# A fused graph-attention and expert kernel: dense experts in the slot pass take two node blocks at a time, in halves of the inner width

## The reference

```python
h = (x_flat @ W_gat).reshape(M, HEADS, NUM_EXPERTS)
a_src = (h * att_src).sum(-1)
a_dst = (h * att_dst).sum(-1)
e = leaky_relu(a_src[src] + a_dst[dst], 0.2)          # one per edge and head
ee = exp(e - segment_max(e, dst)[dst])
agg = segment_sum(h[src] * ee / denom, dst)           # 16 numbers a node
scores = layernorm(agg + b_gat).reshape(M, 4, 4).mean(1)
topk_s, topk_i = top_k(scores, 2); w = softmax(topk_s)
for ei in range(4):                                   # dense: every node, every expert
    g = where(topk_i == ei, w, 0).sum(-1)
    hh = gelu(x @ W1[ei] + b1[ei])                    # 256 -> 512
    out = out + g[..., None] * (hh @ W2[ei] + b2[ei]) # 512 -> 256
```

## Time and profile before

| | |
|---|---|
| Median of 3 runs | 7682.64 us (7681.4 to 7688.64) |
| The profiled execution | 7684.64 us, with a span of 7682.9 us in the trace |
| Slot pass, first gather to last sums | 6160.9 to 7561.8 us of the span |
| Behind it (scores and mixing) | to the end at 7682.9 us |

### The profile page before, as it was taken

One profiled execution on the slowest core, in us unless ns is written; L12 is line 12 of the kernel. 1 busy time (PEld: TensorE's weight loads), 2 busy tenths in 40 slices (PEclk: granted clock), 3 DMA queues, 4 the chain that ended last, 5 costly groups with the idle time before them and its releaser, 6 DMA issues. The chain is left out here.

```text
span 7682.9 us, 117784 instructions
## 1 busy us (share of the span) xinstructions
PE 5447.3 (71%) x27644; PEld 4598.9 (60%) x27645; DVE 3924.1 (51%) x10109; ACT 1568.1 (20%) x3440; POOL 5707.3 (74%) x7330
## 2 busy tenths in 40 slices
PE   3888888777772599990555555555556589999993
PEld 3666666666661489880444434344435589999983
DVE  4777777888887500005454544444445533333326
ACT  1222222222220233330000000000001234444431
POOL 2888888888876577776888888888886577777762
PEclk7888888888885699995777777776777678888886
DMA  3333333333333255553333333333331133333698
GB/s 121 106 106 106 106 107 105 103 103 103 102 101 95 85 174 174 171 172 117 104 104 104 102 92 92 92 92 92 92 93 49 28 86 79 80 79 80 71 72 188
DMA packets 426071, 793.43 MB, mean 103 GB/s; under 512 B 129162, under 2 KB 267134, under 8 KB 425684
## 3 DMA queue, kind: packets, MB, share of 16 engines
q0 software_dynamic: 235504, 474.87, 26.8%
q1 hardware_dynamic: 190436, 317.20, 12.2%
HBM read 720.67 MB, written 70.98 MB: 103 GB/s over the span
## 5 line engine op out<-in xcount | busy, mean ns | idle before, releaser
L1156 PE MATMUL g_pM<-g_G,g_S 128*128 x3328 | 1196.6, 537 | 1190.0 <-ACTq L1050 1070.9
L834 POOL DMA_INDIRECT g_G<-table,X x1664 | 1611.4, 968 | 401.9 <-issue 385.6
L845 POOL DMA_INDIRECT g_G<-table,g_IDX x1616 | 1542.1, 954 | 416.7 <-issue 392.3
L1156 PEld LDWEIGHTS g_pM<-g_G,g_S 128*128 128x128 f32 x3328 | 916.0, 282 | 1470.5 <-issue 1272.4
L1124 PE MATMUL g_pM<-g_G,g_S 128*128 128x260 f32 x3328 | 1125.3, 481 | 407.5 <-DVE acc L953 400.6
L618 POOL DMA_INDIRECT slots<-sort_PAIR,sort_ADDR x1024 | 1029.1, 1005 | 415.4 <-issue 276.2
L1699 POOL DMA_INDIRECT q_G<-table,slot x1072 | 1028.3, 959 | 370.3 <-issue 320.6
L961 DVE TENSOR_TENSOR acc<-g_pM,acc 128x256 f32 x1664 | 698.4, 420 | 1005.4 <-PE g_pM L1156 1002.6
L1124 PEld LDWEIGHTS g_pM<-g_G,g_S 128*128 128x128 f32 x3328 | 706.5, 231 | 692.7 <-DVE acc L953 566.5
L953 DVE TENSOR_TENSOR acc<-g_pM,acc 128x260 f32 x1664 | 711.2, 427 | 188.8 <-PE g_pM L1124 40.4
L941 DVE TENSOR_SCALAR g_S<-iota,g_REL,g_WT 128x128 f32<-128x128 f32 x1664 | 591.2, 356 | 193.2 <-issue 172.4
(11 more groups left out here) (336 smaller groups left out, 7382.3 us busy)
## 6 DMA issues: line engine op xcount, KB each, us to landing
e_W<-in_L_ffn_W SPq DMA_DIRECT2D x210, 512.0 KB, 4.4
sort_PAIR<-slot_rows SPq DMA_DIRECT2D x66, 512.0 KB, 4.5
g_G<-table,X POOLq DMA_INDIRECT x1664
g_G<-table,g_IDX POOLq DMA_INDIRECT x1616
ys_all<-ew_Y SPq DMA_DIRECT2D x196, 128.0 KB, 1.8
sm_Y<-ys_all SPq DMA_DIRECT2D x28, 896.0 KB, 10.6
q_ST<-slot_rows SPq DMA_DIRECT2D x34, 512.0 KB
sort_ADDR<-slot_rows SPq DMA_DIRECT2D x34, 512.0 KB
```

The costliest lines, as they stand in the source:

```text
L834: pool.indirect_dma_start(G[:, r, u, :], None, table, bass.IndirectOffsetOnAxis(ap=IDX[:, k * GRP + u:k * GRP + u + 1].bitcast(U32), axis= ...
L845: pool.indirect_dma_start(G[:, r, u, :], None, table, bass.IndirectOffsetOnAxis(ap=IDX[:, g * GRP + u:g * GRP + u + 1].bitcast(U32), axis= ...
L1156: m = pe.matmul(pM[r % 2 * 2 + half][:, u % HG, :], S[:, r, u, :], rows.rearrange("p a d -> p (a d)"), start=True, stop=True)
```

## The change

A dense unit is now two blocks by one expert, done in two halves of the inner width. `by_w1` of a half covers 2 of the 4 chunks for two blocks: 4 matmuls of 256 columns, with one weight load for the two blocks. `gelu` of a half is 2 activations of 128x256. `by_w2` of a half adds its 2 chunks to both blocks' outputs, 4 matmuls of 256 columns, in one PSUM bank that holds 512 columns and is complete after the second half. `add_b2` and `store` come once for two halves, with 128x512 and 256 KB. The 49 blocks make TWOS = 25 twos; the last is blocks 47 and 48, so block 47 is computed twice and stored once. Halves stand where pairs stood: one in an even group and two in an odd one. A loop body has 16 groups with 24 halves, the loop has 7 passes where there were 15, and `REST` gives two halves to each of the first four groups of the last six.

```diff
-        self.GT = layer.sb(f"{tag}_GT", [P, 2, HC, P])
-        self.Y = layer.sb(f"{tag}_Y", [P, E, D])
+        self.GT = layer.sb(f"{tag}_GT", [P, 2, HC // 2, 2 * P])
+        self.Y = layer.sb(f"{tag}_Y", [P, E, 2, D])
...
-    def by_w1(self, pe, i, e):
-        q = i * self.E + e
-        n = len(self.pH)
-        at_least(pe, self.s["gelu"], (q + 1 - n) * self.HC)
-        for c in range(self.HC):
+    TWOS = (NB + 1) // 2
+    HALF = 2
+
+    def first_block(self, two):
+
+        return NB - 2 if isinstance(two, int) and two == self.TWOS - 1 else two * 2
+
+    def by_w1(self, pe, two, e, half):
+        q = (two * self.E + e) * 2 + half
+        at_least(pe, self.s["gelu"], (q - 1) * self.HALF)
+        for c in range(self.HALF):
+            hidden = (half * self.HALF + c) * P
+            out = self.pH[half][:, c, :].rearrange("p (a m) -> p a m", a=2)
             for k in range(KC):
-                m = pe.matmul(self.pH[e % n][:, c, :], self.W1[:, e, k, c * P:(c + 1) * P],
-                              self.XT[:, bass.ds(i, 1), k, :].rearrange("p a m -> p (a m)"), start=(k == 0), stop=(k == KC - 1))
+                m = pe.matmul(out, self.W1[:, e, k, hidden:hidden + P], self.XT[:, bass.ds(self.first_block(two), 2), k, :],
+                              start=(k == 0), stop=(k == KC - 1))
         m.then_inc(self.s["h"], 1)
 
-    def by_w2(self, pe, i, e):
-        q = i * self.E + e
-        n = len(self.pY)
-        at_least(pe, self.s["yc"], q + 1 - n)
-        pe.wait_ge(self.s["gelu"], (q + 1) * self.HC)
-        for c in range(self.HC):
-            m = pe.matmul(self.pY[e % n][:, 0:D], self.GT[:, e % 2, c, :], self.W2[:, e, c, :], start=(c == 0),
-                          stop=(c == self.HC - 1))
+    def by_w2(self, pe, two, e, half):
+        q = (two * self.E + e) * 2 + half
+        if half == 0:
+            at_least(pe, self.s["yc"], two * self.E + e - 1)
+        pe.wait_ge(self.s["gelu"], (q + 1) * self.HALF)
+        for j in range(2):
+            for c in range(self.HALF):
+                m = pe.matmul(self.pY[e % 2][:, j * D:(j + 1) * D], self.GT[:, half, c, j * P:(j + 1) * P],
+                              self.W2[:, e, half * self.HALF + c, :], start=(half == 0 and j == 0 and c == 0),
+                              stop=(half == 1 and c == self.HALF - 1), skip_group_check=True)
         m.then_inc(self.s["y"], 1)
 
-    def gelu(self, a, i, e):
-        q = i * self.E + e
+    def gelu(self, a, two, e, half):
+        q = (two * self.E + e) * 2 + half
         a.wait_ge(self.s["h"], q + 1)
         at_least(a, self.s["y"], q - 1)
-        for c in range(self.HC):
-            a.activation(self.GT[:, e % 2, c, :], self.pH[e % len(self.pH)][:, c, :], ACT.Gelu,
-                         bias=self.B1T[:, e * self.HC + c:e * self.HC + c + 1]).then_inc(self.s["gelu"], 1)
-
-    def add_b2(self, v, i, e):
-        q = i * self.E + e
-        v.wait_ge(self.s["y"], q + 1)
-        at_least(v, self.s_stored[e], i * 16)
-        v.tensor_tensor(self.Y[:, e, :], self.pY[e % len(self.pY)][:, 0:D], self.B2[:, e, :], ALU.add).then_inc(self.s["yc"], 1)
-
-    def store(self, sp, i, e):
-        sp.wait_ge(self.s["yc"], i * self.E + e + 1)
-        sp.dma_start(self.ys[bass.ds(i * P + e * NP, P), :], self.Y[:, e, :]).then_inc(self.s_stored[e], 16)
+        for c in range(self.HALF):
+            at = e * self.HC + half * self.HALF + c
+            a.activation(self.GT[:, half, c, :], self.pH[half][:, c, :], ACT.Gelu,
+                         bias=self.B1T[:, at:at + 1]).then_inc(self.s["gelu"], 1)
+
+    def add_b2(self, v, two, e):
+        v.wait_ge(self.s["y"], (two * self.E + e) * 2 + 2)
+        at_least(v, self.s_stored[e], two * 16)
+        v.tensor_tensor(self.Y[:, e], self.pY[e % 2][:, :].rearrange("p (a d) -> p a d", a=2),
+                        self.B2[:, e, :].unsqueeze(1).broadcast_to([P, 2, D]), ALU.add).then_inc(self.s["yc"], 1)
+
+    def store(self, sp, two, e):
+        sp.wait_ge(self.s["yc"], two * self.E + e + 1)
+        if isinstance(two, int) and two == self.TWOS - 1:
+            r0 = e * NP + (NB - 1) * P
+            sp.dma_start(self.ys[r0:r0 + P, :], self.Y[:, e, 1, :]).then_inc(self.s_stored[e], 16)
+        else:
+            sp.dma_start(self.ys[bass.ds(two * (2 * P) + e * NP, 2 * P), :].rearrange("(a p) d -> p a d", p=P),
+                         self.Y[:, e]).then_inc(self.s_stored[e], 16)
...
-    STEP = 2 * RINGS
+    STEP = 4 * RINGS
     FULL = SGF // STEP
     E = dense.E
-    PAIRS = [[0], [1, 2], [3], [4, 5], [6], [7, 8], [9], [10, 11]]
-    REST = [[0], [1], [2], [3], [], []]
-    NPAIR = sum(len(x) for x in PAIRS)
+    HALVES = [[n // 2 * 3] if n % 2 == 0 else [n // 2 * 3 + 1, n // 2 * 3 + 2] for n in range(STEP)]
+    REST = [[0, 1], [2, 3], [4, 5], [6, 7], [], []]
+    NHALF = sum(len(x) for x in HALVES)
...
+        def halves(it, g):
 
             if not exists(it, g):
                 return []
-            table_of = REST if isinstance(it, int) and it == FULL else PAIRS
+            table_of = REST if isinstance(it, int) and it == FULL else HALVES
             return [(it, m) for m in table_of[g]]
 
-        def block_expert(it, m):
-            return it * (NPAIR // E) + m // E, m % E
-
-        def pair_before(it, m):
-
-            return (it, m - 1) if m > 0 else (it - 1, NPAIR - 1)
+        def unit(it, m):
+            return it * (NHALF // (2 * E)) + m // (2 * E), m // 2 % E
+
+        def second(it, g):
+
+            return [unit(*half) for half in halves(it, g) if half[1] % 2 == 1]
+
+        def half_ahead(it, m):
+
+            return (it, m - 1) if m > 0 else (it - 1, NHALF - 1)
...
-                for pair in pairs(*later(it, g, -2)):
-                    dense.store(sp, *block_expert(*pair))
+                for of in second(*later(it, g, -2)):
+                    dense.store(sp, *of)
...
-                for pair in pairs(it, g):
-                    dense.by_w1(pe, *block_expert(*pair))
-                    if not (isinstance(it, int) and it == 0 and pair[1] == 0):
-                        dense.by_w2(pe, *block_expert(*pair_before(*pair)))
+                for half in halves(it, g):
+                    dense.by_w1(pe, *unit(*half), half[1] % 2)
+                    if not (isinstance(it, int) and it == 0 and half[1] == 0):
+                        ahead = half_ahead(*half)
+                        dense.by_w2(pe, *unit(*ahead), ahead[1] % 2)
                 if exists(*later(it, g, -1)):
...
-                    dense.by_w2(pe, *block_expert(FULL, REST[g - 1][0]))
+                    dense.by_w2(pe, *unit(FULL, REST[g - 1][-1]), 1)
```

More of the change, by code:

```diff
@@ L1617, in slot_pass @@
         pN = sc.ps(f"{tag}_pN", [P, P])
-        pH = [sc.ps(f"{tag}_pH{j}", [P, dense.HC, P]) for j in range(2)]
+        pH = [sc.ps(f"{tag}_pH{j}", [P, dense.HALF, 2 * P]) for j in range(2)]
         pY = [sc.ps(f"{tag}_pY{j}", [P, 512]) for j in range(2)]
@@ L1647, in round_of @@
             return it * (STEP // RINGS) + g // RINGS
-        def pairs(it, g):
+        def halves(it, g):
             if not exists(it, g):
                 return []
-            table_of = REST if isinstance(it, int) and it == FULL else PAIRS
+            table_of = REST if isinstance(it, int) and it == FULL else HALVES
             return [(it, m) for m in table_of[g]]
-        def block_expert(it, m):
-            return it * (NPAIR // E) + m // E, m % E
-        def pair_before(it, m):
-            return (it, m - 1) if m > 0 else (it - 1, NPAIR - 1)
+        def unit(it, m):
[4 more added lines that the diff above has]
+            return (it, m - 1) if m > 0 else (it - 1, NHALF - 1)
         def chunk(c):
@@ L1689, in _ @@
             for e in range(E):
-                sp.wait_ge(dense.s_stored[e], NB * 16)
+                sp.wait_ge(dense.s_stored[e], dense.TWOS * 16)
         @block.gpsimd
@@ L1747, in step @@
                     onehots(*later(it, g, 1))
-                for pair in pairs(*later(it, g, -2)):
-                    dense.add_b2(v, *block_expert(*pair))
+                for of in second(*later(it, g, -2)):
+                    dense.add_b2(v, *of)
                 v.wait_ge(s["pcol"], k + 1)
@@ L1765, in step @@
                 a.activation(G[:, r, :, HE:width], ARG[:, g % 2], ACT.Exp).then_inc(s["pcol"], 1)
-                for pair in pairs(it, g):
-                    dense.gelu(a, *block_expert(*pair))
+                for half in halves(it, g):
+                    dense.gelu(a, *unit(*half), half[1] % 2)
             over_groups(a, step)
```

## The result

The changed kernel takes 7709.56 us in the median of 12 runs (7695.99 to 7729.74), the kernel before 7680.96 (7674.18 to 7688.64): a ratio of 1.0037 with a 95% interval of 1.0028 to 1.0046. It is slower, by 28.6 us, where 7683 was forecast. Its runs also spread over 34 us where those of before spread over 14.

A forecast was written before the change was run, and what follows sets the result against it. POOL's gathers were taken to bind up to 7198, their landing behind it. The profiled 7684.6 us, -4 for matmuls and +5 for block 47, gave 7685.6; the median lies 2.0 lower, hence 7683, range 7668 to 7704.

The forecast's parts named there:

- the second rival: In the slot pass's loop, the longer body is not kept and returns wait for instructions: +18 us, 7701, chance 0.12.
- What bounds the pass: Slot pass up to 7198: POOL issues gathers almost without a break, 10.06 us a group, and PE follows at that pace.
- First-layer matmuls: by_w1 in 8 wide records saves 0.06 us a pair; -4 us up to 7198, bounds 0 and -6.8.
- The tail follows the landing of gathers: Behind 7198 gathers land at 11.1 us a group, which the change leaves alone: 0 us, other bound -27.3.
- Block 47 twice: At the slot pass's end, two units instead of one in groups 128 to 131: +5 us, bounds +2 and +9.
- Gelu, bias, stores: In the dense units: gelu stays covered, bias saves 0.14 us for two halves on DVE, stores move the same bytes; no cost.
- First rival, PE binds after all: In the slot pass, PE sets the pace, so all waits beyond the gap go: 7654 us, chance 0.12.
- Third rival, the clock falls more often by itself: In the slot pass, PE's mean clock falls to 0.84 and groups take 10.3 us: 7708 us, chance 0.08.

The follow-up runs named there:

- a_step64: The changed kernel with 64 groups written out and 64 in a loop of one pass; 7698.03 us against 7695.13 for the kernel before, 1.0004.
- a_again_c: The changed kernel run again, unedited; 7734.86 us with the kernel before at 7698.81, ratio 1.0044.
- a_step8: The changed kernel's units with a body of 8 groups, experts taken two by two in two loops; 7699.39 us, 1.0000 of the kernel before.
- a_step8_last1: The changed units with a body of 8 groups in two loops, the last two computing block 48 alone; 7697.5 us, 0.9994 of the kernel before.
- b_step16: The kernel before with only its loop body lengthened to 16 groups, 7 passes instead of 15; 7739.82 us, 1.0042 of the kernel before.

## Why the prediction was wrong

The step that failed: the sum that gave 7683 (-4 for the matmuls, +5 for block 47) has no term for the loop's body. It took the longer body to be kept, which put the returns at nothing, and left their cost to the second rival, "the loop's body no longer stays with PE", with a chance of 0.12. The runs showed six returns with stalls of 27.0 us in all, 29.7 us more of POOL's waits, and a time 28.6 us longer; with a short body the same units cost nothing (1.0000). The rival's mechanism was right: 0.08 MB of body are kept and the new body is not, no q8 packets before and some after, stalls at the returns, and the sign. Its chance, its count and its size were off.

Its chance. The rows showed only that 0.08 MB stay, and nothing on what 0.13 MB would do (by the packets it is 0.16). No row spoke for their staying; the 0.12 came from no evidence, and with the sum of all other terms near zero this one unknown decided the sign.

Its size. I took 3.9 us for each of 7 returns, 27 in all, and let PE's saving and the rings take back a third, for 18 and a time of 7701. There are six returns, of 4.5 us on average; that the product is 27.0 again is luck. What was wrong is the taking back: more was lost behind the stalls than I had counted, and the rings do not take back a fixed part of it. The first spread behind each stall takes 2.96 to 3.57 us where it takes 1.8 at full clock, some 9 us over the six. And POOL's waits are spread unevenly. Behind the first stall, which began when POOL was just ending a wait of 3.42 us, it waits 15.4 us in 4 times up to 6560 (in 6500 to 6560 of before it is 1.0 in one); behind the third and fourth, of 3.10 and 2.87 us, it does not wait for PE at all until 7186. So the price of a return hangs on how far PE is ahead when it comes.

The clock decides that in part, and it is low in stretches that the stalls do not make. Windows of 10 us around the first return (busy us of PE, PEld, DVE, ACT and POOL, then the granted clock, the DMA share and GB/s):

```profile
6490.00:6500.00 10.00, 10.00 (x40) 8.70 (x40) 3.20 (x7) 2.12 (x3) 7.56 (x9) 0.66 0.14 15
6500.00:6510.00 10.00, 4.97 (x32) 4.64 (x30) 0.29 (x1) 2.35 (x4) 5.32 (x6) 0.88 0.37 88
6510.00:6520.00 10.00, 10.00 (x42) 8.76 (x41) 3.41 (x8) 3.87 (x6) 3.07 (x3) 0.61 0.06 4
6520.00:6530.00 10.00, 10.00 (x41) 8.69 (x41) 2.75 (x7) 1.89 (x3) 7.19 (x8) 0.66 0.47 139
6530.00:6540.00 10.00, 10.00 (x52) 9.09 (x51) 3.35 (x8) 3.63 (x5) 4.71 (x6) 0.75 0.08 5
6540.00:6550.00 10.00, 10.00 (x49) 8.97 (x48) 2.94 (x8) 2.35 (x4) 7.28 (x8) 0.67 0.38 88
```

PE is busy all the time behind the stall, but at a mean clock of 0.61 to 0.75 for 40 us, where it needs 0.86 to keep POOL's pace. That is not all the stall's doing: the clock stood at 0.66 already in the 10 us ahead of it, and `a_step64`, with the same units and no return, has the same fall in the midst of unbroken work:

```profile
6520.00:6530.00 10.00, 10.00 (x62) 9.17 (x62) 2.70 (x7) 4.47 (x7) 7.75 (x8) 1.00 0.55 139
6530.00:6540.00 10.00, 10.00 (x55) 9.09 (x55) 3.35 (x8) 3.64 (x5) 7.64 (x8) 0.75 0.13 10
6540.00:6550.00 10.00, 10.00 (x38) 8.40 (x38) 3.16 (x7) 2.86 (x5) 7.59 (x8) 0.74 0.35 87
6550.00:6560.00 10.00, 10.00 (x47) 8.87 (x47) 2.93 (x7) 3.97 (x7) 7.56 (x9) 0.66 0.36 89
6560.00:6570.00 10.00, 10.00 (x48) 8.92 (x47) 2.24 (x7) 2.12 (x3) 7.56 (x9) 0.66 0.52 140
```

Behind the sixth return, the longest stall of all, the clock is back at 1.00 after ten us of work:

```profile
7360.00:7370.00 10.00, 10.00 (x42) 8.95 (x42) 3.19 (x7) 2.90 (x4) 0.00 (x0) 0.61 0.61 7
7370.00:7380.00 10.00, 10.00 (x62) 9.17 (x61) 2.80 (x7) 4.80 (x8) 7.03 (x7) 1.00 0.76 138
```

And in the second trace of the changed kernel, `a_again_c`, the first return stalls PE by 2.96 us, the clock is 1.00 again from 6530 to 6560, and POOL waits 1.5 us for PE in 3 times in 6500 to 6600. So a stall by itself costs little more than the first work behind it at 1.2 GHz, and the nearest reading is that the first return was dear because it fell into a low stretch with PE already late. The Trainium skill (TensorE: Matmul & The Clock Gate, HAM oscillation) says that an idle gap between bursts of matmuls brings the clock down and that the price is paid again at each burst. The trace agrees for the work right behind each stall; the low stretches of 40 us are not of that kind, as PE is busy throughout. The uneven price would also fit the wider spread of the changed kernel's runs. That this spread has this cause is argued, not shown.

Two small slips of the working changed nothing: -6.8 + 2 around the median gives 7678 as the lower end of the forecast's own range, not 7674, and the work of a group is 8.68 us by the rows, not 8.66.

The other points, one by one:

- *What bounds the pass.* Right. With the fetching gone (`a_step8`, `a_step64`), POOL waits for PE about 1 us beyond the ordinary gap up to the tail, and the whole kernel is no faster than before: POOL's pace is the floor.
- *First-layer matmuls: -4 us, bounds 0 and -6.8.* Right in the traces: 6.8 us of waits became 1.2 in `a_step8`, 0.7 in `a_step64` and 3.9 in `a_step8_last1`, one trace each. In the medians it does not show (1.0000, with an interval of 0.1%).
- *The tail follows the landing of gathers.* Half right. It takes the same 27 groups in 300 us after the change, as line L1755 alone shows (compare):

```profile
7220.00:7520.00 300.00, 5.08 (x27) 0.84 0.89 70
```

  But POOL's waits there grew from 31.5 to 42.2 us, and one of them is 11.4 us, behind the return that stalls PE by 10.01 us. A wait as long as that is not absorbed. `a_step8` has 34.1 us there in 16 waits, close to before.
- *Block 47 twice: +5.* Not resolved, see above.
- *Gelu, bias, stores: nothing.* Nothing of them shows in the time. An activation of 256 columns takes 471 ns against 369 for 128, and a bias of 512 columns 680 against 411 for 256:

```profile
L1516 ACT ACTIVATE ew_GT<-q_pH,ew_B1T 128x256 f32<-128x256 f32 x332 | 139.4, 471 | 339.3 <-PE q_pH L1494 338.7
L1522 DVE TENSOR_TENSOR ew_Y<-q_pY,ew_B 128x512 f32<-128x512 f32 x82 | 55.8, 680 | 39.1 <-PE q_pY L1505 39.1
```

- *First rival, PE binds after all.* False: taking PE's lateness away up to the tail in `a_step8` brought no gain beyond these few us. The 25 ns more for a narrow matmul, which the prediction took from the Trainium skill (TensorE: Matmul & The Clock Gate, Back-to-back issue gap), are not in this kernel: 8 wide records of the first layer now take 1.73 us (7556.50 to 7558.23, and as much in the second layer, 7558.23 to 7559.96), where 16 narrow ones took 1.79. Sixteen times 25 ns would be 0.4 us:

```profile
7556.50 1.89 PE L1494 MATMUL q_pH<-ew_XT,ew_W 128*128 128x256 f32 x8
7558.23 1.89 PE L1505 MATMUL q_pY<-ew_W,ew_GT 128*128 128x256 f32 x8
7559.96 1.86 PE L1818 MATMUL slot_sums<-q_G,q_S 128*128 128x20 f32 x16
```

- *Third rival, the clock falls more often by itself.* False: the mean from 6200 to 7200 is 0.86 in the changed kernel against 0.87, and with the same units and no costly returns it is 0.89 (`a_step8`, `a_step64`).

## What to carry to other kernels

When a change makes a loop's body longer, look at the instruction queues of the profile over the loop: if they are silent, the body is kept, and a longer one must be shown to be kept too. Here 8 groups (0.08 MB) were kept and 16 (0.16 MB in the changed kernel, 0.18 with the old units) were not; where between them the limit lies was not tried. A regrouping of the same work that kept the body at 8 groups took the whole loss away. Code that ran straight through cost nothing that can be measured (1.0004), so here writing the groups out was safer than a body that is too long. Count the returns, not the passes.

Fewer and wider matmuls are worth what the rows of both widths say: where the narrow ones already run at the pace of their columns, as here (112 against 108 ns for 128 columns of float32), there is next to nothing to gain but instructions.

## What the runs showed of the hardware

- A return to a loop body that is no longer kept stalls PE by 2.4 to 5.0 us, and the sixth return in each of three traces (the changed kernel twice, `b_step16` once) by 9.3 to 10.0 us; it falls in the tail, where the DMA engines are busy for 0.8 to 0.9 of the time. That the packets of instructions have to stand behind the gathers' there was not tried.
- The same code fetched in order, 58 packets of 16 KB, showed no wait of PE for it.
- The first spread behind a stall of 2.5 to 10.0 us ran at about 1.2 GHz (2.96 to 3.57 us, not 1.8). Apart from that the clock falls in stretches of some 40 us while PE is busy without a break: 1.00 to 0.66 in `a_step64` between 6530 and 6570.
- The kernel before took 7681 to 7699 us in three sets of runs and 8907 and 9052 in two others, on one core, all stages slower and with "issue" waits on PE, DVE and ACT; a few tenths of a per cent cannot be judged there.
